# Layer 1's state in one eviction or in two column halves, in a three-layer interaction network

## What is computed

```python
x0 = inputs
prev = inputs
for i, f in enumerate(CIN_LAYERS):          # [128, 128, 128]
    h = prev.shape[1]
    Wr = Ws[i].reshape(h, M, f)
    z = relu(einsum('bhk,bmk,hmf->bfk', prev, x0, Wr) + bs[i][None, :, None])
    half = f // 2
    results.append(z[:, :half])
    prev = z[:, half:]
pooled = sum(concatenate(results, axis=1), axis=-1)
return pooled @ W_lin
```

## Time and profile before

| | us |
|---|---|
| median of 3 runs | 1955.07 |
| lowest and highest of them | 1955.04, 1956.12 |
| the profiled execution | 1955.95 |
| its span, first to last instruction | 1954.1 |
| TensorE busy | 1948.5 |
| VectorE busy | 1884.1 |
| ScalarE busy | 649.7 |
| GpSimd busy | 256.3 |

### The profile page before, as it was taken

The page is one execution under the profiler, slowest core; times in us unless marked ns, Lnnn a source line. Parts: engine busy times, 40 slices in busy tenths (PEclk is TensorE's granted clock), DMA queues, the critical chain, the costliest instruction groups (busy, mean ns, idle before and its releaser), DMA issues.

```text
span 1954.1 us, 31455 instructions
## 1 busy us (share of the span) xinstructions
PE 1948.5 (100%) x10864; PEld 786.4 (40%) x10864; DVE 1884.1 (96%) x1329; ACT 649.7 (33%) x760; POOL 256.3 (13%) x298
## 2 busy tenths in 40 slices
PE   9999999999999999999999999999999999999999
PEld 3333444444444444444444344444444434444333
DVE  8989999999999999999999999999999999999988
ACT  2332234432244322344223442224432244422332
POOL 1001101111011111111111111101111111111000
PEclk9999999999999999999999999999999999999999
DMA  7998987788887889878798778987879878789710
GB/s 166 191 195 173 199 173 163 163 176 189 182 173 154 174 174 196 175 151 175 161 202 180 155 167 165 199 189 150 169 166 191 193 156 166 164 178 201 149 40 1
DMA packets 139165, 326.42 MB, mean 167 GB/s; under 512 B 34001, under 2 KB 60010, under 8 KB 139141
## 3 DMA queue, kind: packets, MB, share of 16 engines
q1 hardware_dynamic: 98051, 294.66, 68.4%
q0 software_dynamic: 40320, 31.21, 11.1%
q10 hardware_dynamic: 770, 0.23, 0.1%
HBM read 294.72 MB, written 0.01 MB: 151 GB/s over the span
## 4 chain that ended last, share of the span: by engine, by line
PE 97%; DVE 1%; ACT 0%; DMA 0%; ACTq 0%; issue 0%; DVEq 0%
PE acc L874 32%; PE acc L753 23%; PE acc L953 19%; PE acc L879 17%; PE acc L942 2%; PE acc L745 2%; PE acc L820 1%; PE acc L960 1%; DVE prod L424 1%; PE acc L967 1%; DMA bias<-b 0%; ACT prev L1095 0%; PE acc L760 0%; ACTq L1192 0%; DVE prod L426 0%
## 5 line engine op out<-in xcount | busy, mean ns | idle before, releaser
L424 DVE TENSOR_TENSOR prod<-prev,x_bc 128x2048 f32<-128x2048 f32 x511 | 1142.4, 2286 | 38.1 <-PE acc L960 22.5
L874 PE MATMUL acc<-prod,w_sb 128*64 128x512 f32 x2912 | 659.5, 593 | 0.0
L953 PE MATMUL acc<-prod,w_sb 128*64 128x512 f32 x1064 | 461.3, 592 | 0.0
L960 PE MATMUL acc<-prod,w_sb 128*64 128x512 f32 x728 | 344.4, 592 | 0.0
L874 PEld LDWEIGHTS acc<-prod,w_sb 128*64 128x64 f32 x2912 | 203.8, 137 | 343.5 <-issue 310.4
L1141 ACT ACTIVATE diff<-acc 64x256 f32<-64x256 f32 x56 | 21.3, 380 | 794.2 <-PE acc L879 793.5
L879 PE MATMUL acc<-prod,w_sb 128*64 128x256 f32 x1344 | 282.6, 379 | 0.0
L1057 ACT ACTIVATE prev<-acc,bias 32x1024 f32<-32x1024 f32 x252 | 279.1, 1108 | 3.6
L753 PE MATMUL acc<-x_rot,w_sb 128*64 128x512 f32 x1240 | 277.5, 593 | 0.0
L426 DVE TENSOR_TENSOR prod<-prev,x_bc 128x1024 f32<-128x1024 f32 x193 | 230.0, 1219 | 10.1 <-ACT prev L1041 10.1
L953 PEld LDWEIGHTS acc<-prod,w_sb 128*64 128x64 f32 x1064 | 144.4, 137 | 219.8 <-issue 179.5
(11 more groups left out here) (98 smaller groups left out, 1203.3 us busy)
## 6 DMA issues: line engine op xcount, KB each, us to landing
x_bc<-x SPq DMA_DIRECT2D x312, 256.0 KB, 13.8
x_bc<-x SPq DMA_DIRECT2D x124, 512.0 KB, 20.6
x_rot<-x SPq DMA_DIRECT2D x155, 312.0 KB
x_rot<-x SPq DMA_DIRECT2D x217, 156.0 KB
x_bc<-x SPq DMA_DIRECT2D x124, 128.0 KB, 8.8
x_rep<-x SPq DMA_DIRECT2D x62, 192.0 KB
x_bc<-x_bc POOLq DMA_DIRECT2D x84, 128.0 KB, 3.3
x_t<-x SPq DMA_DIRECT2D x64, 128.0 KB, 9.2
```

The source lines that it names most:

```text
L424: mul = nc.vector.tensor_tensor(prod[:, s:s + w, :], twice, x_bc[:, u, t:t + w, :], ALU.mult)
L874: mm = nc.tensor.matmul(acc1[f, h, :], w[:, f], prod[:, s, BANK * h:BANK * h + BANK], start=False, stop=stop, skip_group_check=closed)
L953: nc.tensor.matmul(acc2[0:HALF, u, :], w, prod[:, s, 0:BANK], start=(pos == 1), stop=False)
L960: mm = nc.tensor.matmul(acc2[HALF:P, u, :], w, prod[:, s, BANK:NB], start=(pos == 1), stop=False)
```

## The change

`evacuate1_by_half` goes, and the 28 paired blocks call `evacuate1`. ScalarE no longer writes the two copies of column half 0 and their part of `prev_t1` while TensorE still works on half 1; it waits for layer 1's last chunk and then writes both copies with 1024 columns each, both parts of `prev_t1`, and the turned copy and the sums as before. The semaphore `half_full` and its increment behind TensorE's last matmul of half 0 go too. TensorE's matmuls and VectorE's instructions keep their order.

```diff
                 for pos in range(BY_HALF, CH):
                     pe.wait_ge(prod_ready, runs + RUN_OF_PAIRED[pos] + 1)
-                    mm = one_half(w1_sb[:, ORDER_PAIRED[pos], :], pos % RING, 0, pos == CH - 1)
-                mm.then_inc(half_full, 1)
+                    one_half(w1_sb[:, ORDER_PAIRED[pos], :], pos % RING, 0, pos == CH - 1)
                 pe.wait_ge(mix_added, i - 1)
...
-            def evacuate1_by_half(i, a, used):
-                for h in range(NH):
-                    cols = slice(BANK * h, BANK * h + BANK)
-                    if h == 0:
-                        act.wait_ge(half_full, i - 1)
-                    else:
-                        act.wait_ge(chunk_used, used + RING)
-                    for g in range(2):
-                        op = nc.scalar.activation(prev[1][0][HALF * g:HALF * g + HALF, cols], acc1[HALF:P, h, :], ACT.Relu,
-                                                  bias=bias[HALF:P, 1:2])
-                    if h == 1:
-                        op.then_inc(prev_ready[1], 1)
-                    spread_t1(h, acc1, 1, a)
-                spread_turned(prev[1], acc1, 1)
-                keep01(acc1, 1, a)
...
-                    evacuate1_by_half(i, u, i * (2 * CH) + CH)
+                    evacuate1(i, u, i * (2 * CH) + CH)
```

More of the change, by code:

```diff
@@ L213, in cin_kernel @@
         mix_added = sem("mix_added")
-        half_full = sem("half_full")
         folded01 = sem("folded01")
```

## The result

The changed kernel takes 1959.32 us (median of 21 runs, 1958.55 to 1959.99), the kernel before beside it 1955.76 us (21 runs, 1955.02 to 1956.34). The ratio is 1.0018, with a 95% interval of 1.0012 to 1.0024: 3.6 us slower. The forecast was 2.5 us slower. The profiled execution has a span of 1957.5 us.

The account below looks back on a forecast made before the run. TensorE, busy 1948.5 of 1954.1 us, was taken to bound the kernel. A 0.64 us delay less ring and TensorE slack left 0.18 us per pair of blocks; 14 x 0.18 = 2.5, 1955.07 + 2.5 = 1957.6 us, range 1955.0 to 1960.2.

Parts of the forecast that it names:

- The bound, and ScalarE's own work: TensorE sets the time; 0.51 us less ScalarE work per block, 14 us over 28, lies in idle time, worth 0.
- The odd block costs nothing: Odd block: state ready at 1087.60, VectorE comes at 1087.82; hidden with 0.22 us over and 1.28 us of ring wait behind.
- The delay in the even block: Layer 2's first product on VectorE, even block: starts at 1028.40 instead of 1027.76, 0.64 us late.
- when the state is ready, even block: After layer 1, even block: ScalarE released at 1026.14, 2.26 us handover from the start-up, so product at 1028.40.
- rival B: Slower by over 0.2%: even ring slack only 0.32 us, or handover 0.1 us longer than 2.26; 1959.5 us, chance 0.16.
- The signs that hung on the handover: Even block: product 2.26 us behind ScalarE's L1041, VectorE idle 0.56 us before it; two blocks 0.18 us longer.
- The ring takes up 0.40 us: VectorE's product-ring wait, even block: slack 0.32 + 0.08 = 0.40 us, so 0.24 of 0.64 us go through.
- TensorE has 0.04 to 0.07 us in hand: End of layer 2, even block: early weight load absorbs 0.04 to 0.07 us, leaving a loss of 0.17 to 0.20.
- One loss per pair, 14 of them: No second loss at the odd block's mix, later ScalarE outputs have cover; 14 x 0.18 = 2.5 us.
- The sum: Whole kernel: 1955.07 + 2.5 = 1957.6 us, +0.13%.
- the likeliest case: Whole kernel: same as before within about 0.2% (3.9 us), chance 0.79.
- The rule of the Trainium skill: Splitting an unsaturated engine's instructions may let others go sooner; predicted to agree in sign for even blocks, not odd ones.

Follow-up runs that it names:

- e1_split_even: Kernel before, but only the 14 even blocks still evict by column halves, the odd ones as a whole; 1955.76 us against 1955.78 (1.0000).
- e5_single_wait: Changed kernel, but layer 2's first product in paired blocks waits only for the state, not its ring slot; 1958.08 us against 1955.97 of before (1.0011).
- e3_wait_on_product: Changed kernel, but layer 2's first product waits for the ring slot first and the state second; 1959.08 us against 1955.78 of before (1.0017).
- e4_wait_and_weigh: e3_wait_on_product with VectorE's small weighing operation moved ahead of layer 2's first product in even blocks; 1958.06 us against 1955.78 of before (1.0012).
- e7_vector_late_even: Kernel before plus 12 tiny VectorE memsets ahead of layer 2's first product in even blocks; 1955.56 us against 1955.97 (0.9999).

## Why the prediction was right, and where it was off

- **The bound, and ScalarE's own work.** Right: less work on ScalarE bought nothing. 0.51 us per block were forecast, which is 14 us; the trace has 12.5, mostly since the time in which short evictions overlap had been counted twice as work.
- **The odd block costs nothing.** Right: no wait for ScalarE there, a ring wait of 1.22 us (1.2 to 1.3 forecast), and `e1_split_even` at the time of before.
- **The delay in the even block: 0.64 us forecast, 0.74 measured.** This step, "when the state is ready, even block", was mis-sized. The 2.26 us were taken from the start-up, where the waits are on constants and the one for the state is on the product itself. In the loop a register operation stands between the wait and the product, and the handover takes 2.36; `e5_single_wait` takes the operation and the second wait out and gets 2.27 and, with 2.1 us over before, about the time that the forecast had named. The prediction had this as half of rival B ("the handover takes 0.1 more than 2.26, since a VectorE that was stopped does not run on as before"), with the right size and only a vague cause, and named 0.28 us of loss per pair as the point from which it decides. It came to 0.26, so the case stayed on the near side of it. That is luck in part: with the prediction's own other terms the delay of 0.74 gives 0.74 - 0.40 - 0.06 = 0.28, the deciding point itself, and only because TensorE had a little more in hand than counted did it stay below. The signs that hung on the handover (product 2.26 us behind the eviction's start, 0.56 us idle, 0.18 us more per pair) came out as 2.36, 0.66 and 0.26.
- **The ring takes up 0.40 us.** Right: the ring wait of the even block is gone and L423 starts 0.08 ahead of its predecessor's end, which is what the 0.40 had counted on beside the printed 0.32.
- **TensorE has 0.04 to 0.07 us in hand.** The mechanism was right, the size just above its upper end: d - loss is 0.48 in six kernels, so it is 0.48 - 0.40 = 0.08. The matmul that starts with its load and takes 0.64 us is there in the trace.
- **One loss per pair, 14 of them.** Right: the mix of the odd block costs nothing more, ScalarE is through 1.06 us ahead of layer 0's state, the leftover product doesn't wait.
- **The sum.** 14 x (0.74 - 0.48) = 3.6 us; 3.6 measured, against 14 x 0.18 = 2.5. The result is within 0.2% of before, as the likeliest case had it, and at 1959.32 near the upper end of the range. The 3.6 us lie inside the forecast of 1.5 to 3.8, but above the 14 x 0.24 = 3.4 that the prediction called its upper bound with nothing in hand on TensorE, which shows that the error lies in the delay. Of the 1.75 us between 1955.07 + 2.5 and 1959.32, 1.06 is the loss and 0.69 the base: the forecast started from the median of three runs, 1955.07, and 21 runs of the kernel before have 1955.76.
- **The rule of the Trainium skill** ("Perfetto Trace Analysis", section "Optimizing Scalar/DVE Operations"), that breaking up instructions of an engine with time to spare may let work be done sooner where it causes bubbles elsewhere: the runs agree for the even blocks, where the split saves 14 waits of 0.66 us on VectorE and 3.6 us of time. They show no gain in the odd ones (1955.76 against 1955.78 us), where VectorE comes to the product later than either form of the state.

## What to carry to other kernels

Where a result is handed from one engine to the next, follow the lateness to the first wait of the receiver that was there already: that idle time, and what the bounding engine holds ready behind it, is what may be lost for nothing, and here all above it was lost in full. A handover time is best taken from a place with the same kind of waits; inside a loop, a register operation or a second wait ahead of the waiting instruction adds to it. Splitting an eviction paid here only in the blocks where the receiver would otherwise have been waiting.

## What the runs showed of the hardware

- A VectorE instruction behind a wait for the state starts 0.03 us behind the end of the eviction where the wait is its only one, 0.10 behind it where a second wait puts a semaphore instruction ahead of it, and 0.13 where a register operation stands between wait and instruction (`e5_single_wait`, `e3_wait_on_product`, the changed kernel).
- A weight load may come 0.34 us behind the start of the matmul ahead with no loss, in a step of 0.43 us. At 0.45 us (`e4_wait_and_weigh`) and at 0.66 (the changed kernel) the matmul starts with its load, takes 0.64 instead of 0.59 us, and the next step is longer by 0.05.
- Twelve memsets of 128x5 took 0.23 us together, although each is listed with 62 ns (`e7_vector_late_even`): they start about 15 ns apart and overlap for most of their length, so a row's mean says little about what another one adds.
